# Small heads in quarter steps: the mask of the first product by TensorE, plain maxima over two heads, bf16 parts subtracted inside their bank

## What is computed

```python
# stage A, layer 1 self-attention: 16 heads of 16, causal
# stage B, layer 1 cross-attention: 16 heads of 16, not causal, int8-rounded activations, biases
# stage C, layer 2 self-attention: 32 query heads of 8, 8 key/value heads, causal
q, k, v = x @ wq, src @ wk, src @ wv             # per head
s = (q @ k.T) * scale                            # scale 0.25, 0.25, 1/sqrt(8)
s = where(causal, s, -inf)                       # A and C
p = softmax(s)                                   # over 256 keys
y = x + (p @ v) @ wo
```

## Time and profile before

| | before |
|---|---|
| median of three runs | 2813.8 us |
| profiled execution | 2822.94 us (span 2820.9 us) |
| TensorE busy | 2207.2 us, 78% of the span |
| VectorE busy | 1722.4 us, 61% |
| ScalarE busy | 1036.5 us, 37% |
| GpSimd busy | 814.9 us, 29% |
| mean granted TensorE clock | 0.835 of 2.4 GHz |

### The profile page before, as it was taken

How to read it: one execution, slowest core, us unless ns; L and a number is a source line. 1 busy time by engine, 2 the same in 40 slices (tenths; PEclk the granted TensorE clock), 3 DMA queues, 4 the chain that set the end, 5 groups by cost and what they waited for, 6 DMA issues and landing times.

```text
span 2820.9 us, 37045 instructions
## 1 busy us (share of the span) xinstructions
PE 2207.2 (78%) x12500; PEld 1564.5 (55%) x12509; DVE 1722.4 (61%) x4967; ACT 1036.5 (37%) x2368; POOL 814.9 (29%) x1357
## 2 busy tenths in 40 slices
PE   6889946886777468785459899689999999898792
PEld 4777824553453245543126576367777776675571
DVE  4655477544554956654867888656666666664532
ACT  2233313321221323222455756244544454443230
POOL 2122222221011213331000000145555555553344
PEclk9999968766786567756569999899999999999896
DMA  6000000000000030000000000200000000005453
GB/s 224 20 17 15 1 15 1 1 1 1 1 1 24 1 159 2 1 1 32 0 0 1 1 1 1 84 1 1 5 1 4 1 1 1 8 5 198 75 140 96
DMA packets 35051, 80.54 MB, mean 29 GB/s; under 512 B 4880, under 2 KB 21776, under 8 KB 32240
## 3 DMA queue, kind: packets, MB, share of 16 engines
q1 hardware_dynamic: 30016, 65.46, 6.3%
q0 software_dynamic: 4560, 12.46, 2.1%
q10 hardware_dynamic: 288, 0.26, 0.0%
HBM read 65.71 MB, written 10.35 MB: 27 GB/s over the span
## 4 chain that ended last, share of the span: by engine, by line
PE 23%; DVE 16%; ACT 6%; POOL 5%; issue 4%; DMA 1%; POOLq 0%; DVEq 0%; SPq 0%; ACTq 0%
PE ps L2085 4%; PE ps L2104 3%; DVE K L2519 3%; PE ps L2851 2%; DVE K L2508 2%; PE ps L2462 2%; POOL C L2735 2%; DVE K L2498 1%; ACT K L2654 1%; PE ps L2431 1%; PE ps L2455 1%; DVE X L1916 1%; ACT K L2655 1%; POOL K L3122 1%; PE ps L2872 1%
## 5 line engine op out<-in xcount | busy, mean ns | idle before, releaser
L1124 ACT ACTIVATE K<-ps 128x768 f32<-128x768 f32 (+1 forms) x128 | 110.4, 863 | 289.9 <-PE ps L967 289.6
L2133 DVE TENSOR_TENSOR_SCAN W<-W,ps 128x512 f32<-128x512 f32 x128 | 155.9, 1218 | 42.1 <-issue 24.5
L1076 DVE CUSTOM_DVE_ANT_0 K<-ps,K 128x128 bf16<-128x128 f32 (+1 forms) x384 | 114.4, 354 | 100.8 <-PE ps L952 100.2
L2085 PEld LDWEIGHTS ps<-K 128*128 128x128 f32 x1024 | 136.9, 196 | 65.8 <-issue 51.9
L2654 ACT ACTIVATE K<-ps,K 128x256 f32<-128x256 f32 x128 | 60.8, 475 | 304.0 <-DVE K L2498 304.0
L2462 PE MATMUL ps<-W,K 128*128 128x256 f32 x512 | 132.6, 405 | 41.9 <-DVE K L2519 35.3
L2730 POOL TENSOR_TENSOR K<-K 128x512 f32<-128x512 f32 x128 | 133.3, 1041 | 108.7 <-DVE K L2501 107.1
L2455 PE MATMUL ps<-W,K 128*128 128x512 f32 x256 | 125.4, 612 | 28.6 <-DVE K L2519 28.6
L2085 PE MATMUL ps<-K 128*128 128x128 f32 x1024 | 139.2, 280 | 8.1 <-DVE W L2133 8.1
L952 PE MATMUL ps<-K 32*128 32x256 bf16 (+1 forms) x1280 | 105.9, 307 | 49.0 <-DVE K L1076 35.7
L2462 PEld LDWEIGHTS ps<-W,K 128*128 128x128 f32 x512 | 100.3, 201 | 67.1 <-DVE K L2519 46.6
(11 more groups left out here) (521 smaller groups left out, 5775.2 us busy)
## 6 DMA issues: line engine op xcount, KB each, us to landing
W<-in_m SPq DMA_DIRECT2D x32, 256.0 KB, 4.6
results<-K SPq DMA_DIRECT2D x63, 128.0 KB
W<-in_wproj SPq DMA_DIRECT2D x1, 4096.0 KB, 12.6
W<-in_m SPq DMA_DIRECT2D x32, 128.0 KB, 5.1
W<-in_Wq SPq DMA_DIRECT2D x1, 2048.0 KB, 12.5
W<-in_Wo SPq DMA_DIRECT2D x1, 2048.0 KB, 16.8
W<-in_w SPq DMA_DIRECT2D x2, 1024.0 KB, 18.3
W<-K SPq DMA_DIRECT2D x4, 512.0 KB, 2.9
```

Source lines behind the costliest of these rows:

```text
L1076: m = e.tensor_tensor_reduce(self.junk[p][:, j, c0:c1], self.ps[j][:, c0:c1], self.maskq[:, m0:256], -1.0, -PAD, ALU.add, ALU.min, to[:, j ...
L1124: e.activation(to, made, ACT.Exp).then_inc(*self.up("exp"))
L2085: m = e.matmul(ps[1 + 2 * (n % 2)][:, b * 128:(b + 1) * 128], self.dtuT[h][:, i, b * 128:(b + 1) * 128], self.diag[s % 4][:, b * 128:(b + ...
L2133: e.tensor_tensor_scan(self.st[i % 3], self.a[i % 3], ps[1 + 2 * (i % 2)][:, :], 0.0, ALU.mult, ALU.add).then_inc(*sig.up("m scan"))
```

## The change

All three stages go from head steps to quarter steps: q = 4s to 4s+3, where even quarters hold the scores of a half step and odd ones its logits. Every engine walks over the quarters.

- Units stand two to four quarters apart (`UNITS` has their quarters) and alternate between banks 5 and 6. Rows, maxima rows and norm turns all go to bank 7, in one order ("rest", "kept").
- A q or k unit's bf16 parts are made without the f32 copy: the bank is read out in bf16 (`LEVELS`: by ScalarE, then by VectorE, then by ScalarE), TensorE adds minus that part to the bank through a scaled identity (`minus`, 128 columns of weights, 512 bf16 columns moved), and the bank is read again. One level per quarter. This is two such matmuls for a unit, three for the keys of C.
- The scale of q moves into the exponential.
- In the causal stages, TensorE writes the mask into both score banks ahead of the scores (identity times the bf16 mask, 2 x 128 columns each, two matmuls per half step), and VectorE takes the maxima with two plain reductions over both banks (2 x 128 and 2 x 256 elements) in place of four fused operations.
- The values of step s-1 are made in the second quarter of step s, ahead of the second half, not after it.
- GpSimd: at the first quarter of a step the maxima parts for s+3 (every second step), at the last quarter the affine select of s. Before, the affine select of s came first.
- The norm turns of a batch's two tiles are one step apart.

```diff
     def schedule(self):
...
-                at.append((b * self.per + self.UNIT_STEPS[i], "unit", unit[0], b, unit[1]))
...
+                at += [(4 * (b * self.per + 4 * r + 5) + 2 * i, "turn", 2 * b + i, r) for i in range(2)]
+            at += [(4 * (end + 2) + 2 * i, "flip", 2 * b + i, 0) for i in range(2)]
+            at += [(4 * (end + 3) + 2 * i, "project", 2 * b + i, 0) for i in range(2)]
+            if self.nx.turned:
+                at += [(4 * (end + 5 + i) + 1, "norm", 2 * b + i, 0) for i in range(2)]
+        at += [(8 * n - 1, "max", n, 0) for n in range(self.N // 2)]
...
     def pe(self, t):
+        for q in self.quarters:
+            s, p, second = q // 4, q % 4 // 2, q % 2
+            if not second and 0 <= s + self.LEAD < self.N:
+                self.pe_scores(t, s + self.LEAD, p)
+            if second and 0 <= s < self.N:
+                self.pe_probabilities(t, s, p)
+            for u, kind, b, c, n in self.units.get(q, ()):
+                if n == 0:
+                    if u >= 2:
+                        self.wait_part(t, u - 2, self.last[u - 2])
+                    m = self.unit(t, kind, b, c, self.ps[5 + u % 2])
+                else:
+                    self.wait_part(t, u, n - 1)
+                    t.wait_ge(self.s("minus"), 1)
+                    m = t.e.matmul(self.ps[5 + u % 2][:, :], self.minus[self.LEVELS[kind][n - 1][2]], self.part(u, kind, b, c, n - 1),
+                                   start=False, stop=True, skip_group_check=True)
+                m.then_inc(*self.up("unit"))
+            if q % 4 == 1 and 0 <= s - 1 < self.N:
                 self.pe_values(t, s - 1)
+            for kind, b, c, u in self.plan.get(q, ()):
+                t.wait_ge(self.s("kept"), u)
+                m = self.pe_rest(t, kind, b, c)
...
     def pe_scores(self, t, s, p):
...
+        if self.CAUSAL:
+            for j in range(2):
+                t.e.matmul(self.ps[j][:, :].rearrange("p (i n) -> p i n", n=256)[:, :, 0:128], self.g.identb,
+                           self.g.maskb.rearrange("p (i n) -> p i n", i=1).to_broadcast([128, 2, 128]), start=True, stop=False,
+                           skip_group_check=True)
...
     def dve(self, v):
...
+        for q in self.quarters:
+            s, p, second = q // 4, q % 4 // 2, q % 2
+            if not second and 0 <= s + self.LEAD < self.N:
+                self.maximum(v, s + self.LEAD, p)
+            self.copy_parts(v, q, "dve")
+            if q % 4 == 1 and 0 <= s - 1 < self.N:
                 v.wait_ge(self.s("quads"), s)
...
+    def copy_parts(self, eng, q, who):
+        for u, kind, b, c, n in self.units.get(q, ()):
+            to, by, _ = self.LEVELS[kind][n]
+            if by == who:
+                eng.wait_ge(self.s("unit"), self.made[u, n])
...
+                self.copy_part(eng, u, kind, b, c, n, self.ps[5 + u % 2]).then_inc(*self.up("parts of " + who))
...
     def maximum(self, v, s, p):
...
-            for j in range(2):
-                for i, (c0, c1, m0) in enumerate(((0, 128, 128), (128, 384, 0))):
-                    m = e.tensor_tensor_reduce(self.junk[p][:, j, c0:c1], self.ps[j][:, c0:c1], self.maskq[:, m0:256], -1.0, -PAD,
-                                               ALU.add, ALU.min, to[:, j, i:i + 1])
+            for i, (c0, c1) in enumerate(((0, 128), (128, 384))):
+                m = e.tensor_reduce(to[:, :, i:i + 1], banks.rearrange("p (j k) -> p j k", j=2)[:, :, c0:c1], AX.X, ALU.max, negate=True)
...
     def act(self, a):
...
+                e.activation(to, made, ACT.Exp, scale=self.SCALE).then_inc(*self.up("exp"))
+            self.copy_parts(a, q, "act")
...
     def pool(self, p):
...
-            if self.CAUSAL and 0 <= s < self.N:
+            if q % 4 == 0 and 0 <= s + self.LEAD < self.N and (s + self.LEAD) % 2:
+                self.maximum_parts(p, (s + self.LEAD) // 2)
+            if q % 4 == 3 and self.CAUSAL and 0 <= s < self.N:
                 p.wait_ge(self.s("exp"), 2 * s + 2)
...
-    UNITS = [("q", 0), ("k", 0), ("q", 2), ("k", 2), ("v", 0), ("v", 1)]
-    UNIT_STEPS = [-7, -7, -6, -6, -3, -2]
+    UNITS = [("q", 0, -20), ("k", 0, -18), ("q", 2, -16), ("k", 2, -14), ("v", 0, -11), ("v", 1, -9)]
+    MINUS = {"low": 0, "high": 1, "all": -1.0}
+    LEVELS = {"q": [("hi", "act", "low"), (0, "dve", "low"), (1, "act", None)],
+              "k": [(0, "act", "high"), (1, "dve", "all"), (2, "act", None)], "v": [("v", "act", None)]}
...
-    UNITS = [("k", 0), ("q", 0), ("q", 2), ("q", 4), ("q", 6), ("v", 0), ("v", 1)]
-    UNIT_STEPS = [-8, -8, -7, -6, -5, -3, -2]
+    UNITS = [("k", 0, -24), ("q", 0, -22), ("q", 2, -18), ("q", 4, -16), ("q", 6, -14), ("v", 0, -11), ("v", 1, -9)]
+    MINUS = {"half": 0, "odd": 2, "first": 3}
+    LEVELS = {"q": [("hi", "act", "odd"), (0, "dve", "odd"), (1, "act", None)],
+              "k": [("hi", "act", "half"), (0, "dve", "first"), ("mid", "act", "first"), ("last", "act", None)],
+              "v": [("v", "act", None)]}
```

More of the change, by code:

```diff
@@ L880, in schedule @@
         for b in range(B):
-            for i, unit in enumerate(self.UNITS):
-                at.append((b * self.per + self.UNIT_STEPS[i], "unit", unit[0], b, unit[1]))
             end = (b + 1) * self.per
             for r in range(self.per // 4):
-                at += [(b * self.per + 4 * r + 5, "row", "turn", 2 * b + i, r) for i in range(2)]
-            at += [(end + 2, "row", "flip", 2 * b + i, 0) for i in range(2)]
-            at += [(end + 3, "row", "project", 2 * b + i, 0) for i in range(2)]
@@ L898, in s @@
+        self.last = {self.index[kind, b, c]: len(self.LEVELS[kind]) - 1 for q, kind, b, c in units}
+        self.quarters = range(min(self.units), max(self.plan) + 6)
     def s(self, name):
@@ L942, in pe_scores, with project @@
+    def project(self, t, W, x, c, b, bank):
+        for i in range(2):
+            for k in range(2):
+                m = t.e.matmul(bank[:, i * 256:(i + 1) * 256], W[:, k, (c + i) * 128:(c + i + 1) * 128], x[:, k, b * 256:(b + 1) * 256],
+                               start=i == 0 and k == 0, stop=k == 1, skip_group_check=True)
+        return m
     def pe_scores(self, t, s, p):
         b, c = divmod(s, self.per)
-        t.wait_ge(self.s("split"), self.splits(b, c))
+        self.wait_unit(t, "q", b, c // 2 * 2)
+        self.wait_unit(t, "k", b, self.key_unit(c))
```

466 lines of the change are left out of this document (186 added, 280 removed).

## The result

The kernel after takes 2722.3 us (median of four runs, 2721.7 to 2731.6), the kernel before 2812.6 beside it. The ratio is 0.9676, with a 95% interval of 0.9637 to 0.9716: 90 us are gone. The forecast was 2769, a gain of 45. So the direction was right, and the size was half of what came.

A forecast was written before the change was run, and what follows sets the result against it. TensorE, at 0.69, 0.78 and 0.66 of full clock, bounds the main stretches of A (16 heads, causal), B (16, cross) and C (32, causal). Stage totals -12 -21 -11 = -44, rounded -45, give 2769 us; range 2714 to 2825.

The forecast's parts named there:

- What bounds: Main stretches of A, B, C: TensorE bounds, busy 115.2 of 133.7, 121.3 of 150.2, 189.4 of 233.7 us.
- The third thing, bunching: q/k projections of one batch run together, one bank each; the next waits for ScalarE's read-out, 0.69 us idle, VectorE standing still.
- TensorE's work at 2.4 GHz: Main stretches after the change, before any waits: 98 us in A, 105 in B, 151 in C.
- The charges for waits and low clock in A and B: Main stretches: charges added to TensorE's work, giving A 118 us against 133.7 and B 129 against 150.2.
- C's main: C's main stretch: work 151 us, chains 39, units 7, handovers 6, low clock 15; 218 against 233.7.
- The wait that spoke against the change: Even causal steps: affine select queued behind maxima's parts, value products wait; chain 6.7 us in A, 6.4 in C.
- The starts and ends: Before the first exponential nothing covers a unit's levels, 4.4 us against 2.7: A +4, B +0, C +5; ends 0.
- (1): Three stages: waits half hidden, half of 111 us of charges for waits and clock gone; gain 100, median 2714; chance 0.10.
- (2): Three stages: dense work anywhere gives 2.4 GHz, so the 23 us for low clock go; 2746; chance 0.05.
- (3): Causal stages: GpSimd's parts stay slow, 4.6 us instead of 2.4, on 24 even steps; +53, 2822; chance 0.10.
- (4): Three stages: TensorE stays at about 0.7 of its clock, added matmuls paid at half clock; net +52, 2866; chance 0.12.
- (5): Unit levels on TensorE's queue stall it, uncovered also in main stretches; 34 units, +48, 2817; chance 0.10.

The follow-up runs named there:

- bunched: Kernel after with q and k units one quarter apart instead of two to four, v units right behind them; 2792.4 us, ratio 0.9902.
- spread_before: Kernel before with only its projections' steps changed, one unit per head step where two stood together; 2725.6 us, ratio 0.967.
- full_extra: Kernel after plus one unneeded 512-column matmul on 128 rows in each of stage C's 86 quarters without unit work; 2727.1 us, ratio 0.9684.
- row_extra: Kernel after plus one unneeded 512-column matmul on 32 rows in each of stage C's 86 quarters without unit work; 2733.1 us, ratio 0.9712.
- late_values: Kernel after with value products two quarters later, behind the second half as in the kernel before, GpSimd's new order kept; 2672.3 us, ratio 0.9481.
- pool_order: Kernel after with GpSimd doing the affine select first and the maxima's parts behind it, as before the change; 2685.8 us, ratio 0.9518.
- f32_split: Kernel after with q and k units copied out in f32 and split from SBUF, as before the change; 2712.7 us, ratio 0.9627.
- best: Kernel after with mask matmuls, in-bank subtraction and GpSimd's new order undone in A and B, C as in late_values; 2655.0 us, ratio 0.9421.
- order_full_extra: pool_order plus the extra matmuls of full_extra in stage C; 2694.4 us, ratio 0.9561.
- hybrid: A and B as in best, C as in order_full_extra; 2660.1 us, ratio 0.9444.
- no_mask: Kernel after without the mask matmuls in A and C, maxima by four fused VectorE operations per half step as before; 2720.5 us, ratio 0.9656.

## Why the prediction was right, and where it was wrong

**What bounds: right.** TensorE bounded the three stretches and its clock was the second term. The reading that evenly spread full-array work bears on the clock was the key; bunched, A in spread_before, and full_extra against row_extra bear it out. The third thing, bunching, was read rightly too: the waits for the single bank (14.1 us in B's main before), which the sum leaves out, are gone. Its 0.69 us of idle stands ahead of the second row, not the third, and these rows show nothing of VectorE.

**TensorE's work at 2.4 GHz: right.** I had 98, 105 and 151 us. A and B, now near 2.4 GHz, have it busy for 100.2 and 101.5. C, at 0.81, can't tell; in late_values, at 0.96, it is busy for 159.9.

**The charges for waits and low clock in A and B: the step that failed.** I charged 20 us in A (chains 6, units 5, handovers 4, clock 5) and 24 in B (maxima loop 3, units 8, int8 6, handovers 4, clock 3). Measured are main stretches of 106.5 and 108.2, so 8.5 and 3.2 over the work. TensorE is idle for 6.3 and 6.7 us in all, and the low clock costs next to nothing (0.94, 1.00). Of the 44 us charged, 12 came. The stages gained 96 us where I had 44; these two terms are 32 of the 52 between. I had added the chains as if each were uncovered; with two unit banks and quarters between the levels TensorE nearly always has other work, as the value products behind the subtraction at 531.63 show.

**C's main: the sum right, its terms not.** 215.3 against 218. But I had 52 us of waits and 15 of low clock. Measured are 30 us idle, and 34 us by which TensorE's busy time is above my 151. The wait that spoke against the change, GpSimd's parts ahead of the affine select, came as described, its length overcharged (39 for the chains, 14.4 in the row of the wait). Taken away it gave 37.3 us of C's main in late_values, near the 39 charged, 25 of it with the clock, and 17.2 in pool_order's profiled execution, nearly all of it idle time. If the clock did rise for that reason, the 39 was right by two errors that cancel: too long a wait, and no price for what it does to the clock. That the sum for C came within 3 us is luck.

**The starts and ends: mis-sized.** +4, 0 and +5 forecast against +0.4, -5.1 and +2.0; B's end gave 6.0 more where I had 0. The mechanism, that a chain of levels with nothing beside it is longer than one copy, is right and was too small: f32_split took 8.0, 17.0 and 6.3 us off the starts. It stood hidden behind what the new placing gave (spread_before took 6.6, 17.8 and 5.1 us off them), which I had counted as one unit less in A. B I had set at nothing by offsetting it against a moved unit, and it holds the largest cost of the levels and the largest gain of the placing.

**Prices.** The mask took 0.33 us where I had 0.23: over my 92 half steps that is 9 us more than I charged, which the overcharged waits outweighed. A subtraction took the 0.23 that I had in 43 of 54 cases, and 0.32 in the others. The page of before gave me the price of a bf16 matmul only in a run of its own kind. Maxima 1.02 (1.1) and copy 0.69 (0.65) were good.

**Steps.** 7.10 us in A (7.9 forecast), 7.21 in B (8.6), 6.95 in C (7.0).

**The rivals.** (1), 2714, came nearest in time (2722), and by half in mechanism: three quarters of the charges were hidden in A and B, next to none in C. I gave it 0.10 since TensorE was busy only 84% at 2.4 GHz before; in the kernel after it is busy 94% in A's and B's main. (2), clock by busy share alone: row_extra speaks against it. (3), slow parts: they take 2.4 us (534.86 to 537.25 in A), and GpSimd's busy time in C fell from 75.5 to 66.8. (4), clock under 0.75: no main stretch. (5), levels that stall TensorE: not in the main stretches, but in the starts.

**The signs.** Clocks, new idle ahead of the value products and the steps came as listed. The first exponentials of A and C came 0.4 and 2.0 us later, not 4 to 5. One sign of being wrong came in part, "a large gain in B alone": B, without mask and affine select, gave 53.2 of the 96 us. It fits a gain that comes from the placing and the two banks, which B has too.

**Left open.** Why C's clock differs as it does between pool_order (0.83, idle 14 us) and late_values (0.96, idle 18 us): the first comes from an execution 19 us slower than its kernel's median. Two pairs of kernels with the same C hardly differ (late_values and best 178.0 and 178.1 us, both at 0.96; order_full_extra and hybrid 191.8 and 188.7, at 0.96 and 0.98), but no second profile of pool_order's C is there. The two unit banks, and the copies and maxima taken off VectorE, weren't tried by themselves; no_mask bounds the maxima together with the mask at about nothing.

## What to carry to other kernels

Before rewriting operations, look at the granted clock and TensorE's idle time by stretch, and at where the full-array matmuls lie: spreading them evenly is a change of constants and gave 3.3% here, as much as the whole rewrite, by the clock and by shorter waits. A wait of 1 to 3 us on TensorE in a stretch of small tiles may be worth more than its length: two ways of taking it away gave 37 and 50 us where its rows held 18. Read the price of a short matmul from a place where its neighbours are those that it will have. And price a longer chain where nothing covers it, in the starts, apart from the steady part.

## What the runs showed of the hardware

- The wait for GpSimd in C: 13.3 us less of it in the wait row went with 37.3 us less in the stretch (late_values), 25.4 of them busy time at a granted clock of 0.96 in place of 0.81. In pool_order's profiled execution, 19 us above that kernel's median, the same wait went with 17.2 us less, at 0.83.
- Matmuls on 128 rows raised the clock (0.81 to 0.90 by 86 of 512 columns), the same 86 on 32 rows didn't (0.81).
- A stretch with more work on the bound engine was shorter: C's main took 178.0 us with the mask matmuls (and plain maxima by VectorE), 189.5 without them, at 0.96 and 0.80.
- One bf16 matmul of 512 columns held TensorE for 0.22 or 0.23 us ahead of a matmul on the full array (43 times), as in a run of eleven of its kind, and for 0.32 ahead of a tile of 32 rows or 32 columns (11 times).
- The same 193 GpSimd instructions were busy 77.0 us beside VectorE's splits between SBUF tiles, and 66.8 without these.
